# Transformer layer with self-attention, cross-attention and gated feed-forward: the heads of both batches as one stream, V projected four heads at a time, and the cross-attention of both batches in one pipeline ahead of both feed-forward parts

## The chip, the cores and the metric

The kernel runs on one core of one Trainium2 chip. The metric is device time in microseconds (us) from launch to end. TensorE is called PE in the profile, VectorE DVE, ScalarE ACT, GpSimd POOL, and SyncE, which issues most of the DMAs here, SP.

## What is computed

One layer on x of shape (2, 1024, 256), with 16 heads of 64 and a condition of (2, 64, 192):

```
h = layernorm(x, ln1); x = attention(h, h) + x            # self-attention, 1024 keys
h = layernorm(x, ln2); x = attention(h, cond_emb) + x     # cross-attention, 64 keys
h = layernorm(x, ln3); p = h @ ff_w1 + ff_b1              # (2, 1024, 2048)
a, gate = p[..., :1024], p[..., 1024:]
out = a * gelu(gate) @ ff_w2 + ff_b2 + x
```

Attention projects q, k and v to 1024 features, takes the softmax of q k^T / 8 for each head, multiplies by v, and projects back to 256 features. Everything is float32. Products that the kernel takes in fp32r split their operands into a high and a low part and add three terms (hi x hi, lo x hi, hi x lo), which `TERMS` lists.

## The kernel before, in words

Each engine has its own hand-written program, and semaphores tie the programs together. The order on every engine is fixed by these programs. Five tables of numbers place work inside the heads: `BURSTS`, `STEPS`, `TURNS`, `V_SLOT` and the function `proj_at`.

The whole program is a loop over the batch, `for b in range(B)`, on every engine. In each turn of it:

- **LayerNorm 1**: DVE takes statistics of x and centres it (L1000), PE turns the result (L522 `transpose_h`), ACT and DVE split it into hT_hi and hT_lo. While PE waits, it executes transposes without a use (L489 `keep_busy`).
- **First projections**: q and k of the first pair of heads (L534 `project`, six matmuls of 512 columns each), then V of all 16 heads in 16 items of six matmuls of 512 columns (L545 `project_v`). Six of them stand ahead of head 0 (`V_EARLY`), ten in its first five steps (`V_SLOT`). V goes to a scratch tensor in DRAM (SP L294) and comes back one head at a time (SP L239).
- **Heads**: a head is eight steps t, one for each tile of 128 keys. In a step PE makes the scores of 128 keys by 1024 queries (L561, 4 matmuls of 512 columns), DVE takes the row maximum (L1043), ACT the exponential (L840), DVE turns the tile in place (L1048). PE multiplies the tiles of the head before by V in two bursts, after the scores of t=2 and t=4 (L581 `attend`), 128 of its matmuls to a burst, ACT gathers the product (L848), PE projects it out in parts (L593) after t=5, 6, 7 and the next t=0, ACT scales it (L861), POOL adds it to X (L433). At t=7 and t=0 stand the projections of a later pair (L534), split by ACT (L811) and DVE (L1019). SP then moves the split q and k of a pair into the operands of its scores (L206, six transfers a head), in the order of its program: placing, V, weights and `wo` all go through this one queue.
- **After the heads**: PE combines the cross-attention's weights with the condition's keys and values (L614 `make_m`, L621 `make_vw`), LayerNorm 2 is done, then the cross-attention goes over eight tiles as a pipeline: scores of tile t (L722), DVE maximum, difference and sum (L1107 to L1121), POOL multiplies by the inverse sum (L471), PE turns tile t-2 (L732) and multiplies tile t-3 (L741).
- **Feed-forward**: in two halves of 512 tokens with 8 steps each: `SC<-hT` is the product with W1 (L770, 12 matmuls of 512 columns), ACT takes the gelu (L955), DVE multiplies (L1156) and splits (L1160), PE multiplies by W2 (L753, 12 matmuls of 256 columns) two steps later.

PSUM is divided in two score buffers `SC` of two banks each and `W` of four banks (TP[0], TP[1], PV, MISC), which all the rest shares.

## Time and profile before

| | |
|---|---|
| median of 3 runs | 1110.43 us (1109.74 to 1113.83) |
| profiled execution, its own time | 1112.73 us |
| its span (first to last instruction) | 1110.9 us |
| mean granted TensorE clock | 0.988 |
| instructions | 28351 |
| DMA moved | 124.52 MB, mean 112 GB/s |

The predictions of time are made against the profiled execution, whose own time is 1.83 us above its span. The page's line of busy times says how long each engine worked in the span. A window (a stretch from one time to another) gives the same for a part of it, and the timeline the single instructions, with what ended the idle time before them.

### The profile page before, as it was taken

The numbers are of one execution on the slowest core, as the hardware profiler recorded it, in microseconds if no ns is written. First come the engines' busy times: TensorE is split into PE (matmuls) and PEld (weight loads), VectorE is DVE, ScalarE is ACT, GpSimd is POOL, SyncE is SP. The second block draws the span as 40 slices with busy tenths as digits, with TensorE's granted clock in tenths as the row PEclk, the third lists the DMA queues.
The fourth block names the chain that finished last, engine by engine and source line by source line (L and its number), as shares of the span: only waits on it lengthen the run. The fifth ranks groups of instructions, "written<-read, shape, count | busy, mean of one in ns | idle before, by whom it ended". The sixth has DMA issues, their size and how long they took to land.

```text
span 1110.9 us, 28351 instructions
## 1 busy us (share of the span) xinstructions
PE 1051.9 (95%) x12178; PEld 846.3 (76%) x12178; DVE 860.5 (77%) x1024; ACT 600.9 (54%) x1082; POOL 333.0 (30%) x312
## 2 busy tenths in 40 slices
...
GB/s 179 295 227 149 146 116 122 144 118 160 102 157 184 99 47 31 39 67 1 19 53 247 202 117 149 116 133 166 108 130 147 144 130 120 21 19 38 1 20 19
DMA packets 178606, 124.52 MB, mean 112 GB/s; under 512 B 142768, under 2 KB 157616, under 8 KB 174128
## 3 DMA queue, kind: packets, MB, share of 16 engines
...
q14 instruction: 30, 0.25, 0.1%
...
## 4 chain that ended last, share of the span: by engine, by line
PE 67%; issue 15%; DVE 6%; POOL 5%; ACT 4%; SPq 2%; DMA 1%; POOLq 0%; DVEq 0%; ACTq 0%
PE W L581 15%; PE SC L561 13%; PE SC L770 8%; PE W L534 7%; PE W L593 7%; POOL X L433 4%; PE W L753 4%; PE W L741 3%; PE W L545 3%; PE SC L722 3%; ACT OTF L848 2%; SPq L206 2%; ACT PR L840 1%; PE W L732 1%; DVE PR L1000 1%
## 5 line engine op out<-in xcount | busy, mean ns | idle before, releaser
L840 ACT ACTIVATE PR<-SC,nmax 128x1024 f32<-128x1024 f32 x256 | 285.9, 1117 | 237.0 <-DVE nmax L1043 237.0
L1043 DVE TENSOR_REDUCE nmax<-SC 128x1 f32<-128x1024 f32 x256 | 307.6, 1201 | 84.3 <-PE SC L561 84.1
L1048 DVE STREAM_TRANSPOSE PR<-PR 128x1024 f32<-128x1024 f32 x256 | 314.9, 1230 | 0.2
L561 PE MATMUL SC<-QKS 128*128 128x512 f32 x1024 | 299.8, 419 | 11.3 <-ACT PR L840 9.0
L433 POOL TENSOR_TENSOR X<-f_raw,X 128x512 f32<-128x512 f32 x128 | 164.3, 1286 | 475.2 <-ACT f_raw L861 474.9
L561 PEld LDWEIGHTS SC<-QKS 128*128 128x128 f32 x1024 | 185.0, 188 | 80.9 <-ACT PR L840 24.6
L581 PE MATMUL W<-PR,V 32*64 32x256 f32 x8192 | 238.7, 377 | 0.5 <-issue 0.5
L581 PEld LDWEIGHTS W<-PR,V 32*64 32x64 f32 x8192 | 186.5, 131 | 46.5 <-issue 13.6
L593 PE MATMUL W<-wo,OTF 128*128 128x256 f32 x512 | 134.2, 385 | 7.8 <-ACT OTF L848 6.0
L593 PEld LDWEIGHTS W<-wo,OTF 128*128 128x128 f32 x512 | 93.6, 189 | 36.4 <-ACT OTF L848 20.0
L861 ACT ACTIVATE f_raw<-W,rden 128x256 f32<-128x256 f32 x256 | 106.7, 474 | 2.2 <-PE W L593 2.0
L1156 DVE SCALAR_TENSOR_TENSOR PR<-SC,b,PR 128x512 f32<-128x512 f32 x32 | 24.0, 750 | 69.2 <-ACT PR L955 69.2
L955 ACT ACTIVATE PR<-SC,b 128x512 f32<-128x512 f32 x32 | 22.1, 689 | 79.2 <-PE SC L770 79.1
L1019 DVE SCALAR_TENSOR_TENSOR QKT<-W,QKT 128x512 fp32r<-128x512 f32 x64 | 43.5, 685 | 13.2 <-ACT QKT L811 13.0
L931 ACT ACTIVATE PR<-PR 128x1024 f32<-128x1024 f32 x16 | 16.9, 1059 | 66.3 <-DVE PR L1111 66.3
L741 PE MATMUL W<-QKT,PT_hi 128*128 128x256 f32 x256 | 50.8, 299 | 0.0
L840 ACT ACTIVATION_READ_ACCUMULATOR PR<-SC,nmax 128x1 f32 x256 | 49.8, 195 | 0.0
L811 ACT ACTIVATE QKT<-W 128x512 fp32r<-128x512 f32 x64 | 38.2, 601 | 18.4 <-PE W L534 18.4
L534 PE MATMUL W<-hT_hi,w_hi 128*128 128x512 f32 x128 | 44.4, 428 | 0.8 <-DVE hT_lo L1011 0.8
L471 POOL TENSOR_TENSOR PR<-PR,crec 128x1024 f32<-128x1024 f32 x16 | 30.4, 1899 | 45.4 <-DVE crec L1121 45.4
L741 PEld LDWEIGHTS W<-QKT,PT_hi 128*128 128x128 f32 x256 | 42.3, 203 | 0.0
L848 ACT COPY OTF<-W 128x1024 f32<-128x1024 f32 x32 | 32.5, 1015 | 16.8 <-PE W L581 14.6
...
## 6 DMA issues: line engine op xcount, KB each, us to landing
...
V<-scratch_v SPq DMA_DIRECT2D x128, 256.0 KB, 4.8
QKS<-QKT SPq DMA_DIRECT2D x128, 128.0 KB, 4.7
...
```

Source lines behind the costliest of these rows:

```text
L433: nc.gpsimd.tensor_tensor(xs, f_raw[:, k % 2, :], xs, ALU.add).then_inc(p_x, 1)
L534: last = mm(bank, w_s[l][:, m, k, :], hT[r][:, k, half * BANK:(half + 1) * BANK], start=(c == 0 and k == 0), stop=(c == 2 and k == KD - 1))
L561: last = mm(SC[t % 2][:, cols], QKS[:, 3 * s, t * P:(t + 1) * P], QKS[:, 3 * s + 1 + l, cols], start=(l == 0), stop=(l == 1))
L581: last = mm(W[cols, a, 0:2 * P], V4[s][rows, blk, :], PR[rows, NT * s:NT * s + NT, Q * blk:Q * blk + Q], start=(blk < 2), stop=(blk >= NB ...
L593: last = mm(W[:, OUT_BANK[k], D * i:D * i + D], OTF[:, t * P:(t + 1) * P], wo2[h % 2][:, :], start=True, stop=True)
L741: last = mm((PV, MISC)[(t - 3) % 2][:, 0:D], PT[l][:, (2 * (t - 3) + n // 4) % NPT, (n % 4) * P:(n % 4 + 1) * P], VWx[r][:, n, :], start=( ...
L770: last = mm(SC[f % 2][:, part * BANK:(part + 1) * BANK], W1[l][:, k, col:col + P], hT[m][:, k, r * BANK:(r + 1) * BANK], start=(c == 0 and ...
L840: nc.scalar.activation(PR[:, NT * s + t, :], SC[t % 2][:, :], ACT.Exp, bias=nmax[:, t % 4:t % 4 + 1], accum_out=den[:, s, t:t + 1]).then_i ...
L848: nc.scalar.copy(OTF[:, :].rearrange("p (t a i) -> p a t i", a=4, i=Q), W[:, :, 0:2 * P].rearrange("p a (t i) -> p a t i", i=Q)).then_inc( ...
L861: done = nc.scalar.mul(f_raw[:, k % 2, D * i:D * i + D], W[:, OUT_BANK[k], D * i:D * i + D], rden[:, h % 2, 2 * k + i:2 * k + i + 1])
L1043: V.tensor_reduce(nmax[:, t % 4:t % 4 + 1], SC[t % 2][:, :], AX, ALU.max, negate=True).then_inc(d_max, 1)
L1048: V.transpose(tile, tile).then_inc(d_tr, 1)
```

## The change

The loop over the batch goes from every engine. In its place:

- The 32 heads of both batches (`HS`) are one stream. Pair g of 16 (`GS`) is projected from places given in `PROJ_AT`. Pairs 8 and 9, the first of batch 1, are projected in heads 13 to 16.
- V is projected in eight units of four heads (`US`). A unit has four items of 12 matmuls with 256 columns each. Unit 0 stands ahead of head 0, the others go one item to a head into the step after the scores of t=5 (`V_AT`); unit 4, the first of batch 1, has its four items in heads 14 and 15. SP stores an item (`store_v`), waits for the four of a unit (`stored`) and loads V for one head (`load_v`).
- LayerNorm 1 of batch 1 is spread over heads 10 to 14: statistics in head 10, aggregation in head 11, the square root on ACT at head 12, centring in head 12, turning and splitting in heads 13 and 14. Statistics of LayerNorm 2 of batch 0 are in heads 29 and 30.
- After the heads, `make_m` and `make_vw` are done for both batches. The cross-attention is one pipeline of 16 tiles. The feed-forward part follows as one loop of 32 steps, whose first two stand in the pipeline's last tiles. `LN_CA` and `LN_FF` place LayerNorm 2 and 3. `keep_busy` is left only at the start.
- W1 and W2 are loaded and split once, W_v comes in pieces of four heads. The gains of LayerNorm 2 and 3 are multiplied on ACT, not on DVE. x of batch 1 is loaded twice (1 MB each).

```diff
+NQ = 4
+def proj_of(g, n):
+    return ((("k", 0), ("q", 0), ("k", 1), ("q", 1)) if g % NP == 0 else
+            (("k", 0), ("k", 1), ("q", 0), ("q", 1)))[n]
+PROJ_AT = {(0, 5): [(1, 0, 3)], (0, 6): [(1, 1, 2)], (0, 7): [(1, 2, 1), (1, 3, 0)],
+           (13, 7): [(8, 0, 3)], (14, 0): [(8, 1, 2)], (14, 7): [(8, 2, 3), (8, 3, 2)],
+           (15, 6): [(9, 0, 2)], (15, 7): [(9, 1, 3)], (16, 0): [(9, 2, 2)], (16, 7): [(9, 3, 3)]}
+for g in range(2, GS):
+    if g not in (8, 9):
+        for n in range(NQ):
+            PROJ_AT[2 * (g - 2) + 1 + n // 2, 7 * (n % 2)] = [(g, n, 2 + n % 2)]
+V_AT = {(0, 4): (1, 0, 0), (14, 5): (4, 0, 3), (14, 6): (4, 1, 0), (15, 0): (4, 2, 0), (15, 5): (4, 3, 3)}
+for u in range(1, US):
+    if u != 4:
+        for i in range(4):
+            if u > 1 or i > 0:
+                V_AT[4 * (u - 1) + i, 5] = (u, i, 3)
+TURN_X = {(13, 0): [(0, 2), (1, 0)], (13, 5): [(2, 3)], (13, 6): [(3, 2)]}
+X_GAIN = {(13, 0): (0, 2), (13, 1): (1, 0), (13, 6): (2, 3), (13, 7): (3, 2)}
+X_HIGH = X_LOW = {(13, 1): 0, (13, 2): 1, (13, 7): 2, (14, 0): 3}
+TURN_W = {(HS - 3, 7): (0, 3), (HS - 2, 0): (1, 2), (HS - 2, 7): (2, 3), (HS - 1, 0): (3, 2)}
...
-V_EARLY = 6
-V_SLOT = {0: (6, 7), 1: (8, 9), 2: (10, 11), 3: (12, 13), 4: (14, 15)}
+LN_CA = {5: 2, 9: 3, 13: 4}
+LN_FF = {3: 5, 11: 6, 19: 7}
...
+def store_v(u, i):
+    sp.wait_ge(a_v, 4 * u + i + 1)
+    sp.dma_start(V_d[u % 2, :, 2 * i:2 * i + 2, :], VST[:, 2 * i:2 * i + 2, :]).then_inc(m_vst[i], 16)
+def stored(u):
+    for i in range(4):
+        sp.wait_ge(m_vst[i], 16 * (u + 1))
...
+for p in range(GS):
+    h = 2 * p
+    if p > 0:
+        for at in ((h - 1, 0), (h - 1, 5)):
+            if at in V_AT:
+                store_v(*V_AT[at][:2])
+        if p == NP - 1:
+            sp.wait_ge(s_tr, 8)
+            sp.dma_start(X[:, 1, :, :], by_row(x, 1)).then_inc(m_xb, 16)
+        sp.wait_ge(s_sc, NT * h)
+        place(p, 1)
+        if p + 2 < GS:
+            load_w(p + 2)
+        if p % 2 == 0:
+            stored(h // 4)
+            sp.wait_ge(s_pv, 8 * (h - 1))
+            load_v(h)
+        elif p // 2 + 2 < US:
+            load_wv(p // 2 + 2)
+        sp.wait_ge(s_op, 4 * (h - 1))
+        load_wo(h)
+        sp.wait_ge(s_pv, 8 * h)
+        load_v(h + 1)
+    if p == 1:
+        load_x(1)
+    for at in ((h, 4), (h, 5), (h, 6)):
+        if at in V_AT:
+            store_v(*V_AT[at][:2])
...
+    if p + 1 < GS:
+        sp.wait_ge(d_qkv, NQ * (p + 2))
+        sp.wait_ge(s_sc, NT * (h + 1))
+        place(p + 1, 0)
...
+    if (h + 2) % 4 and p + 1 < GS:
+        sp.wait_ge(s_pv, 8 * (h + 1))
+        load_v(h + 2)
...
+def project_v(u, i, bank):
+    if i == 0:
+        pe.wait_ge(p_wv, u + 1)
+    for j in range(2):
+        for c, (l, r) in enumerate(TERMS):
+            for k in range(KD):
+                last = mm(bank[:, 4 * DH * j:4 * DH * (j + 1)], hT[l][:, k, (2 * i + j) * P:(2 * i + j + 1) * P],
+                          wv_s[r][:, k, :], start=(c == 0 and k == 0), stop=(c == 2 and k == KD - 1))
+    last.then_inc(s_v, 1)
...
+for h in range(HS):
+    for t in range(NT):
+        scores(h, t)
+        if h > 0 and t in BURSTS:
+            attend(h - 1, BURSTS[t])
+        if h > 0 and t in STEPS:
+            if (h, t) == (NH - 2, 7):
+                pe.wait_ge(a_v, V_ISSUED[h] + 2)
+            project_out(h - 1, STEPS[t])
+        if (h, t) in V_AT:
+            u, i, bank = V_AT[h, t]
             if h == 0:
-                for i in V_SLOT.get(t, ()):
-                    project_v(i)
+                pe.wait_ge(a_v, 4)
+            elif t == 0:
+                pe.wait_ge(a_op, 4 * (h - 2) + 3)
+            project_v(u, i, W[:, bank, :])
...
-    pe.wait_ge(a_op, 4 * (H0 + NH))
-    keep_busy(MISC, 16)
-    pe.wait_ge(d_vw, 4 * b + 2)
-    transpose_h(L2, 0)
-    keep_busy(MISC, 8)
...
+make_m(0, 0, SCB[0])
+make_m(0, 1, SCB[1])
+attend(HS - 1, (0, NB))
+pe.wait_ge(a_exp, HS * NT)
+make_m(0, 2, SCB[2])
+make_m(0, 3, SCB[3])
+pe.wait_ge(d_m, 2)
+turn_z(0, SCB[0:2])
+for k in range(3):
+    project_out(HS - 1, k)
+pe.wait_ge(d_m, 4)
+turn_z(1, SCB[2:4])
+pe.wait_ge(a_op, 4 * (HS - 1) + 2)
+project_out(HS - 1, 3)
+for j in range(4):
+    if j > 0:
+        pe.wait_ge(a_op, 4 * (HS - 1) + (0, 1, 3, 4)[j])
+    make_m(1, j, MB[j])
+pe.wait_ge(a_ln, 2)
+ca_scores(0)
+pe.wait_ge(m_kvb[1], 16)
+pe.wait_ge(m_cao, 16)
+for j in range(4):
+    pe.wait_ge(d_m, 4 + j + 1)
+    make_vw(0, j, MB[j])
+pe.wait_ge(a_ln, 4)
+ca_scores(1)
+for j in range(4):
+    pe.wait_ge(d_vw, j + 1)
+    make_vw(1, j, MB[j])
...
+NC = B * NT
+for C in range(2, NC + 3):
+    if C < NC:
+        pe.wait_ge(d_cs, C - 1)
+        ca_scores(C)
+    elif C < NC + 2:
+        if C == NC:
+            pe.wait_ge(p_f, 8)
+        pe.wait_ge(d_cs, C - 1)
+        ff_up(C - NC)
...
+for F in range(2, B * 2 * NF + 2):
+    if F < B * 2 * NF:
+        pe.wait_ge(d_u, F - 1)
+        if F == 4:
+            pe.wait_ge(p_f, 12)
+        ff_up(F)
+    if F in LN_FF:
+        n = LN_FF[F]
+        if n == 5:
+            pe.wait_ge(d_cx, NC)
+        else:
+            pe.wait_ge(d_fx, 2 * (n - 5))
+        turn_z(n, TP if n == 6 else (PV, MISC))
+    if (F - 2) % NF == 0 and F > 2:
+        pe.wait_ge(a_ln, 2 * (4 + (F - 2) // NF) + 2)
+    ff_down(F - 2)
...
+        if h == NH - 6:
+            if t == 0:
+                for r in range(2):
+                    dve.wait_ge(m_x[r], 32)
+            stats(NT + t, X[:, 1, t, :], d_st)
+        if h == NH - 5:
+            if t == 0:
+                dve.wait_ge(d_st, 2 * NT)
+            aggr(NT + t, d_mv)
+        if (h, t) == (NH - 4, 1):
+            dve.wait_ge(a_sd, 3)
+            V.reciprocal(rs[:, NT:2 * NT], sd[:, NT:2 * NT]).then_inc(d_rs, 1)
+            dve.wait_ge(d_rs, 3)
+        if h == NH - 4 and 2 <= t < 6:
+            for i in (2 * t - 4, 2 * t - 3):
+                centre(X[:, 1, i, :], X[:, 1, i, :], NT + i, d_z)
```

The first place is the middle of a head on PE, after the second burst. Before, scores and output projections alternate (`L593` is the output projection, `L561` the scores, `L534` a projection of q or k):

```order
L581 MATMUL W<-PR,V_0 64x256 x64
L561 MATMUL SC<-QKS 128x512 x4
L593 MATMUL W<-wo_0,OTF 128x256 x2
L561 MATMUL SC<-QKS 128x512 x4
L593 MATMUL W<-wo_0,OTF 128x256 x2
L561 MATMUL SC<-QKS 128x512 x4
L593 MATMUL W<-wo_0,OTF 128x256 x2
```

After, the same place (`L613` is the burst, `L590` the scores, `L625` the output projection, `L575` V):

```order
L613 MATMUL W<-PR,V_1_63 64x256 x64
L590 MATMUL SC<-QKS 128x512 x4
L625 MATMUL W<-wo_1,OTF 128x256 x2
L575 MATMUL W<-wv_hi,hT_hi 128x256 x2
L575 MATMUL W<-wv_lo,hT_hi 128x256 x2
L575 MATMUL W<-wv_hi,hT_lo 128x256 x2
L575 MATMUL W<-wv_hi,hT_hi 128x256 x2
L575 MATMUL W<-wv_lo,hT_hi 128x256 x2
L575 MATMUL W<-wv_hi,hT_lo 128x256 x2
L590 MATMUL SC<-QKS 128x512 x4
L625 MATMUL W<-wo_1,OTF 128x256 x2
```

One item of V, 12 matmuls, has come between the output projection at t=5 and the scores of t=6; nothing else moved there.

The second place is PE after the last head. Before (`L614` is `make_m`, `L581` the whole of the last head's product, `L621` `make_vw`, `L489` `keep_busy`, `L522` the turning of LayerNorm 2, `L722` the first scores of the cross-attention):

```order
L614 MATMUL SC<-V_0,WQT 128x128 x8
L581 MATMUL W<-PR,V_1 64x256 x128
L614 MATMUL SC<-V_0,WQT 128x128 x4
L593 MATMUL W<-wo_1,OTF 128x256 x4
L614 MATMUL SC<-V_0,WQT 128x128 x4
L593 MATMUL W<-wo_1,OTF 128x256 x4
L621 MATMUL SC<-CAW,V_0 128x256 x8
L489 MATMUL W<-ident 128x128 x16
L522 MATMUL SC<-ident,PR 128x128 x8
L489 MATMUL W<-ident 128x128 x8
L722 MATMUL SC<-QKS,hT_hi 128x512 x4
```

After (`L642` is `make_m`, `L553` the turning, `L648` `make_vw`, `L666` the scores of the cross-attention):

```order
L642 MATMUL SC<-KV_0_64,WQT 128x128 x8
L613 MATMUL W<-PR,V_1_63 64x256 x128
L642 MATMUL SC<-KV_0_64,WQT 128x128 x8
L553 MATMUL SC<-ident,PR 128x128 x8
L625 MATMUL W<-wo_1,OTF 128x256 x6
L553 MATMUL SC<-ident,PR 128x128 x8
L625 MATMUL W<-wo_1,OTF 128x256 x2
L642 MATMUL W<-KV_0_64,WQT 128x128 x16
L666 MATMUL SC<-QKS,hT_hi 128x512 x4
L666 MATMUL SC<-QKS,hT_lo 128x512 x2
```

Both halves of LayerNorm 2 are turned between other work, the transposes without a use are gone, and `make_m` of batch 1 (x16) stands ahead of the first scores. `make_vw` of the two batches (x8 each) follows the scores of tile 0 and of tile 1.

The third place is ACT at the start of head 12, where the square root of batch 1's LayerNorm 1 is taken (`L909` is the exponential, `L928` the scaling, `L885` the high part of q or k, `L880` the square root):

```order
L909 ACTIVATE PR_49,den<-SC1,nmax 128x1024
L928 ACTIVATE f_raw<-W,rden 128x256 x2
L885 ACTIVATE QKT2_54<-W 128x512 x2
L880 ACT_TABLE_LOAD
L880 ACTIVATE sd<-mv 128x8
L909 ACT_TABLE_LOAD
L909 ACTIVATE PR_49,den<-SC0,nmax 128x1024
```

Two table loads and the root now stand inside the stream of exponentials; before, they stood between the batches.

## Rows read from the trace of the kernel before

**Rows 1.** The page: busy time, share of the span and instructions of each engine.

```profile
PE 1051.9 (95%) x12178; PEld 846.3 (76%) x12178; DVE 860.5 (77%) x1024; ACT 600.9 (54%) x1082; POOL 333.0 (30%) x312
```

**Rows 2.** Windows: one inner head, then the end of batch 0 to head 1.

```profile
core 0: us, PE busy (x) PEld busy (x) DVE busy (x) ACT busy (x) POOL busy (x), PEclk, DMA share, GB/s
94.61:116.74 22.13, 21.82 (x317) 16.70 (x316) 19.82 (x20) 14.57 (x27) 6.29 (x7) 1.00 0.46 94
...
381.25:407.58 26.33, 25.24 (x565) 20.80 (x564) 16.94 (x18) 12.78 (x25) 6.00 (x5) 1.00 0.25 77
407.58:423.15 15.57, 12.91 (x88) 11.40 (x81) 10.02 (x24) 10.30 (x19) 8.43 (x7) 1.00 0.17 52
423.15:448.47 25.32, 18.54 (x97) 15.51 (x97) 22.88 (x35) 8.88 (x12) 11.17 (x9) 0.93 0.07 21
448.47:474.36 25.89, 25.89 (x178) 23.71 (x176) 20.16 (x25) 6.98 (x10) 17.85 (x17) 1.00 0.11 35
...
490.13:559.84 69.71, 68.24 (x394) 60.01 (x393) 29.52 (x52) 23.27 (x37) 2.39 (x1) 1.00 0.02 8
559.84:588.80 28.96, 22.90 (x114) 19.60 (x113) 17.86 (x43) 8.34 (x14) 15.57 (x16) 0.88 0.35 87
588.80:620.63 31.83, 30.87 (x135) 24.97 (x135) 23.13 (x23) 18.12 (x33) 2.28 (x4) 1.00 1.06 265
...
1106.47:1110.90 4.43, 0.00 (x0) 0.00 (x0) 1.29 (x2) 0.00 (x0) 0.00 (x0) 0.71 0.29 118
```

**Rows 3.** Timeline of PE: start, duration; starts of head 0's and head 11's bursts.

```profile
72.55 3.71 PE L581 MATMUL W<-PR,V 32*64 32x256 f32 x128
...
316.31 3.71 PE L581 MATMUL W<-PR,V 32*64 32x256 f32 x128
```

**Rows 4.** Timeline of PE: one feed-forward step, two products with W1.

```profile
499.24 0.28 PE L753 MATMUL W<-W_hi,PT_hi 128*128 128x256 f32 x1
...
500.68 0.63 PE L770 MATMUL SC<-hT_hi,W_hi 128*128 128x512 f32 x2
...
504.86 0.63 PE L770 MATMUL SC<-hT_hi,W_hi 128*128 128x512 f32 x2
```

**Rows 5.** Timeline of DVE: row maxima of tiles 0 and 8, and two in head 7.

```profile
41.95 1.23 DVE L1043 TENSOR_REDUCE nmax<-SC 128x1 f32<-128x1024 f32 x1 [0.21 <-PE SC L561]
...
68.24 1.22 DVE L1043 TENSOR_REDUCE nmax<-SC 128x1 f32<-128x1024 f32 x1
...
218.66 1.19 DVE L1043 TENSOR_REDUCE nmax<-SC 128x1 f32<-128x1024 f32 x1
...
220.91 1.19 DVE L1043 TENSOR_REDUCE nmax<-SC 128x1 f32<-128x1024 f32 x1
```

**Rows 6.** Timeline of PE: half of `make_m`, `make_vw`, half of a `transpose_h`.

```profile
410.80 1.05 PE L614 MATMUL SC<-V,WQT 128*128 128x128 f32 x8
...
413.42 3.62 PE L621 MATMUL SC<-CAW,V 128*128 128x256 f32 x16
...
495.63 1.04 PE L522 MATMUL W<-ident,PR 128*128 128x128 f32 x8
```

**Rows 7.** Timeline of ACT: a table load and the activation after it.

```profile
493.15 1.28 ACT L955 ACT_TABLE_LOAD   x1 [0.30 <-PE SC L770]
494.45 0.69 ACT L955 ACTIVATE PR<-SC,b 128x512 f32<-128x512 f32 x1
```

**Rows 8.** Timeline of DVE: cross-attention's steady tile, and statistics of four tiles.

```profile
457.93 1.23 DVE L1107 TENSOR_REDUCE cmax<-SC 128x16 f32<-128x1024 f32 x1 [0.80 <-PE SC L722]
...
480.10 1.40 DVE L989 BATCH_NORM_STATS2 st<-X 128x6 f32<-128x256 f32 x4
```

**Rows 9.** Groups by line: weight loads of one operand pair of W2.

```profile
L753 PEld LDWEIGHTS W<-W_lo,PT_hi 128*128 128x128 f32 x128 | 24.5, 191 | 0.9
```

**Rows 10.** Timeline of SP's queue and PE: placing for batch 1's first scores.

```profile
580.54 7.13 SPq L206 DMA_DIRECT2D QKS<-QKT  x6
...
588.80 1.17 PE L561 MATMUL SC<-QKS 128*128 128x512 f32 x4 [1.48 <-DMA QKS<-QKT]
```

More of the change, by code:

```diff
@@ L59, in build_block @@
+        fence = sb("fence", [P, 36 * S])
+        X = sb("X", [P, B, NT, D])
         hT = [sb("hT_hi", [P, KD, S], F32R), sb("hT_lo", [P, KD, S], F32R)]
-        QKS = sb("QKS", [P, 6, S], F32R)
-        V4 = [sb(f"V4_{h}", [P, NB, DH]) for h in range(2)]
         OTF = sb("OTF", [P, S])
@@ new lines, in ff_up @@
+            def ff_up(F):
+                q, f = divmod(F, NF)
+                if f == 0:
+                    pe.wait_ge(d_ll, 2 * (4 + q) + 2)
+                for part, col in enumerate((FF + f * P, f * P)):
+                    for c, (l, m) in enumerate(TERMS):
+                        for k in range(KD):
+                            last = mm(SC[F % 2][:, part * BANK:(part + 1) * BANK], W1[l][:, k, col:col + P],
+                                      hT[m][:, k, by_col(q)], start=(c == 0 and k == 0), stop=(c == 2 and k == KD - 1))
+                last.then_inc(s_ff, 1)
@@ new lines, in ff_down @@
+            def ff_down(F):
+                q, f = divmod(F, NF)
+                pe.wait_ge(d_ul, F + 1)
+                for i in range(4):
+                    bank = ((TP[0], TP[1]), (PV, MISC))[q % 2][i // 2]
+                    for c, (l, m) in enumerate(TERMS):
+                        last = mm(bank[:, D * (i % 2):D * (i % 2) + D], PT[l][:, F % NPT, i * P:(i + 1) * P],
+                                  W2[m][:, f, :], start=(f == 0 and c == 0 and i % 2 == 0),
+                                  stop=(f == NF - 1 and c == 2), skip_group_check=True)
+                last.then_inc(s_w2, 1)
@@ new lines, in ca_exp @@
+            def ca_exp(C):
+                act.wait_ge(d_cs, C + 1)
+                nc.scalar.activation(E[C % 4], E[C % 4], ACT.Exp).then_inc(a_ce, 1)
+            for r in range(2):
+                act.wait_ge(d_mv, 4 * r + 4)
+                root(by_tile(r), a_sd)
+            for r in range(2):
+                for k in range(2):
+                    act.wait_ge(d_h, 2 * r + k + 1)
+                    nc.scalar.copy(hT[0][:, k, by_col(r)], h32[:, k, by_col(r)]).then_inc(a_hh, 1)
+            raw_kv(0)
```

1561 lines of the change are left out of this document (765 added, 796 removed).

## The prediction

> **What bounds the kernel now.** I read the busy times first [rows 1]: PE works 95% of the span, DVE 77%. Of 1110.9 us PE is idle for 59.0, so whatever is to be won beyond that must come from work that is dropped. The windows then say where the idle time is [rows 2]. An inner head lasts 22.13 us, PE busy for 21.82 of it and DVE for 19.82: in the heads PE is the bound, and DVE is close behind. The idle time is elsewhere. From the end of the last head's bursts to the steady cross-attention PE idles 15.57 - 12.91 = 2.66 and 25.32 - 18.54 = 6.78 us, and between the end of batch 0 and its successor's first scores 28.96 - 22.90 = 6.06 us. The reader should also see what that busy time holds: in these stretches PE executes transposes without a use, and its first projections and six V items, while no exponential runs. Head 0 with ten V items takes 31.83 us to the next burst [rows 2], nearly all PE time. The gain of the change is the second start, 28.96 + 31.83 = 60.8 us, and the second entry into the cross-attention, less what is put into the heads.
>
> **The heads.** From the burst of head 0 to that of head 11 are 11 heads in 316.31 - 72.55 us, 22.16 each [rows 3]. The stream has 30 such intervals between the bursts of head 0 and head 30: 30 x 22.16 = 664.8. All but two hold the same two projections as before or the turning of the cross-attention's weights, so I leave them at that.
>
> V is added. In the feed-forward part 12 matmuls of 256 columns, also with loaded weights of 128x128 and three terms, take from 499.24 to 500.68, 1.44 us; the step of 4.18 us less 1.44 leaves 2.74 for 12 of 512 columns, so an item of before costs 1.37 and one of after 1.44 [rows 4]. After unit 0 and the item in head 0, 27 items stand in the stream. Since PE is the bound there, each costs its whole time less the little that it already idles (0.31 us a head [rows 2]): I take 1.43, near the upper bound of 1.44, because the waits in a head are at other places than the V item; the lower bound is 1.44 - 0.31 - the 0.6 or so by which a longer head lets waits on ACT and DVE vanish, about 0.6. The sum is 27 x 1.43 = 38.6. DVE gets nothing of it (V is copied by ACT), and at 23.6 us a head DVE has 3.8 us left.
>
> LayerNorm 1 of batch 1 has four turnings of four transposes in head 13, and the row of two such has 1.04 us with the drain of its last, so some 0.45 each and 1.8 for four [rows 6]. With a wait of 0.4 at each I take 3.4 for all, bounds 1.6 and 6. Its DVE work, eight statistics at 1.40/4 = 0.35 [rows 8] and some 20 more small operations over five heads, lies in DVE's free time. The root at head 12 brings two table loads of 1.28 us, and the activation behind one starts 1.30 us after it [rows 7]. They delay one exponential by about 2.8 us; PE is two tiles ahead of it, with a row maximum every 2.25 us [rows 5], and most of that wait is filled by the projection and output at t=0. I take 0.8, bounds 0 and 2.8. The Trainium skill ("ScalarE: Activation LUTs", section "What ACT_TABLE_LOAD costs") has a switch cost 2.66 us, a load of 1283 ns and a drain of 1380 ns. The row shows the 1.28 and no drain behind it; by the page the sum would be 2.7 us longer, some 1080 instead of 1077. The stream so takes 664.8 + 38.6 + 3.4 + 0.8 = 707.6 us.
>
> **The start.** Before, 72.55 us pass to the first burst [rows 3]. Ahead of head 0 stand four items instead of six, 2 x 1.37 less; its first row maximum is at 41.95 [rows 5] and would come at 39.6 (I give the four items of new form 0.4 more). From tile 0 to tile 8 before are 68.24 - 41.95 = 26.29 us, because two V items stand in each early step; without them DVE sets the pace, with 8 x 2.25 and splits of 0.7 behind two tiles, 19.5. The first burst follows 72.55 - 68.24 = 4.3 us later, as before. Together 39.6 + 19.5 + 4.3 = 63.4; bounds 60 (nothing of the early DMA is late) and 67 (the second placing is late, where the DMA engines now work at a share of 1.06 [rows 2]).
>
> **After the heads.** From head 30's burst to the end of head 31's: 26.33 before [rows 2], 26.3 after. Then to the fifth tile's scores before 15.57 + 25.32 = 40.9 us, of which PE idles 9.4 and has 24 transposes without a use, 0.1 each going by an x8 row less its drain, 2.4. The change adds M and V·W of batch 1: two rows of 1.05, less a drain 0.9 each, and 3.62, less its drain 3.5, 5.3 together [rows 6]. They fit the idle time and the dropped 2.4, but the chain that made PE wait (statistics, root, centring, turning, splitting on DVE) is still there, only earlier: half of its LayerNorm 2 statistics is done in heads 29 and 30. I take 41; bounds 34 (all idle time used) and 46 (nothing hidden). Twelve more tiles at 25.89/4 = 6.5 us [rows 2] are 78.0; three turnings of LayerNorm 2 and 3 at 0.9 [rows 6] are 2.7. DVE idles 0.80 us in a tile [rows 8], and nine extra pieces of DVE work of about 1.4 us each (four centrings of a half, three splits, two statistics of 1.40) are put into the twelve tiles: 12.6 against 9.6 free, so 3.0 of stalls, bounds 0 and 9 x (1.4 - 0.8) = 5.4, up to 10 if a delay also reaches POOL's multiplication. The tail of the pipeline has two turnings at 0.8 and three products of 24 matmuls at 1.44/12 = 0.12 [rows 4], 10.2. The joined feed-forward part is twice 69.71 [rows 2] and 1.8 for two more turnings, 141.2. The end stays 4.4 [rows 2].
>
> Sum: 63.4 + 707.6 + 26.3 + 41.0 + 78.0 + 2.7 + 3.0 + 10.2 + 141.2 + 4.4 = 1077.8, against a span of 1110.9. With the 1.8 us outside the span 1079.6 against the execution's own 1112.7; the median of the runs is 2.3 less, so 1077 us.
>
> What costs nothing: W1 and W2 split once instead of twice spares POOL alone, which is busy for 30% [rows 1]; storing V in 32 pieces, and reading x again, are transfers beside the heads, where the DMA engines have a share of 0.46 [rows 2]. If that cover is gone, the price is rival D's.
>
> **The rivals.**
>
> A. V is paced by its weight loads. One takes 191 ns [rows 9], and an item has 12 now instead of six. If loads of full height didn't overlap more than one deep here, an item would take 12 x 0.191 = 2.29 us, 0.85 more: 32 x 0.83 = 27 us, and 1104. Against it stands the pitch of 0.12 us at which the feed-forward part runs with the same loads [rows 4, 9]. The Trainium skill speaks for it: "TensorE: Matmul & The Clock Gate", section "The mechanism", says that a weight load overlaps running matmuls only where the row group differs, and these all fill the rows. By that rule the stride of 0.12 couldn't be, so the trace disagrees. Chance 0.05.
>
> B. The heads absorb V. If a longer head lets PE's waits on ACT and the weight loads' gaps vanish, an item costs 0.9 to 1.0 instead of 1.43: 27 x 0.48 = 13 less, 1064. For it: the 22.13 us of a head hold only 16.70 of weight loads [rows 2], so the busy PE is not PE at its peak. Against it: it is busy for 21.82 of 22.13. Chance 0.12.
>
> C. The seams cost more: the start at its upper bound (+4), LayerNorm in head 13 and the tables (+4), the entry into the cross-attention (+5), the stalls (+5). Any two or three of them give 1087 to 1095. Chance 0.10, more likely through the cross-attention, where DVE is nearly full.
>
> D. Slower: SP's queue. It places q and k for a head when the head before it has left its slot, issues them for 7.13 us, and the one place where PE was seen to wait for them cost 1.48 us [rows 10]. The queue now has `store_v` ahead of the placing and `stored` ahead of V's loads, and each wait holds all behind it. If placing came late in every head, it costs per head what it is late: at 1.1 us a head the gain of 33 is gone, at 1.3 the kernel is slower by over 0.5%; at 1.48 in 30 heads it is +44, 1121. Against it: the item in step 5 of a head is copied by ACT within two steps, and the placing waits for step 8 anyway; the issue takes 7.13 us of the 23.6 that a slot has, and a landing behind it of as much again still leaves 9. Chance 0.04.
>
> **How the numbers follow.** The forecast has 0.69, so 1077 us. A measurement of this kernel can tell about 0.5%, that is 1105 to 1116 for no change. A, which ends just at that border, gives most of "same" and the upper half of D "slower"; B and C are faster. So faster 0.92, same 0.04, slower 0.04. The range leaves out A and D and the far ends of B and C: below, 1077 less 13 for V and 2 for the start, 1062; above, 1077 and the unknown costs of C together, 20, 1097.
>
> **What would show it.** Right: the interval between bursts in heads 1 to 10 is 23.5 to 23.7 us, V's 12 matmuls take 1.4 to 1.5 from first to next instruction, head 12 is less than 3 us longer, the first burst is at 60 to 67, the pipeline's tiles come every 6.5 to 7 us, the feed-forward step every 4.18. Wrong: the interval at 24.4 or more with weight loads as cause (A); at 23.1 or less (B); DVE as releaser of PE in the cross-attention with tiles of 7 and more (C); the scores waiting for QKS at t=0 or t=4 of many heads (D). A granted clock below the 1.00 of the heads in the stream would also break the sum.

## The result: 3.6% slower, and the profile after

The changed kernel took 1150.92 us (median of 4 runs, 1147.97 to 1156.53) against 1111.97 us (1109.74 to 1113.83) of the kernel before: a ratio of 1.0357, 95% interval 1.0305 to 1.0409. The forecast was 1077 us with a range of 1062 to 1097, and a chance of 0.04 for slower. The forecast missed by 74 us, and the sign with it. The profiled span is 1146.5 us, to be held against the forecast sum of 1077.8.

The page of the changed kernel, busy times:

```profile
PE 1055.1 (92%) x12270; PEld 841.2 (73%) x12270; DVE 859.3 (75%) x997; ACT 605.5 (53%) x1094; POOL 308.4 (27%) x280
```

PE has about the work that it had [rows 1], 1055.1 us against 1051.9. It now idles 91 us instead of 59 (span less busy time). PE's busy time hardly grew, and part of the growth is work at a lowered clock (below); what is new is that PE waits. For what, the view of the waits of PE tells (engine and line that wait, the instruction waited for, us in total, times, longest):

```profile
PE W L565 <- ACT VST L892: 25.5, 24, 1.1
PE W L826 <- POOL PR L498: 14.7, 7, 3.5
PE SC L590 <- ACT PR L909: 11.3, 8, 2.9
PE W L553 <- DVE PT_lo L1296: 7.3, 3, 3.3
PE W L625 <- ACT OTF L917: 6.7, 27, 0.7
PE W L648 <- DVE M_lo L1115: 3.9, 1, 3.9
PE W L613 <- DVE hc L1106: 3.6, 1, 3.6
```

The first row is new in kind and the largest: 24 times 1.1 us, the projection of q or k (L565) waits for ACT's copy of V (L892). The second row is not new: in the kernel before it is `PE W L732 <- POOL PR L471: 15.3, 6, 3.5`. The windows of one inner head, of the interval between bursts that holds the two table loads, of the head with LayerNorm 1 of batch 1, of the entry into the cross-attention, of its tiles 4 to 15, and of the rest:

```profile
core 0: us, PE busy (x) PEld busy (x) DVE busy (x) ACT busy (x) POOL busy (x), PEclk, DMA share, GB/s
...
236.96:261.86 24.90, 23.50 (x330) 18.05 (x329) 19.90 (x20) 14.93 (x28) 8.11 (x9) 1.00 0.72 144
312.07:339.91 27.84, 23.58 (x330) 18.06 (x329) 22.28 (x28) 18.32 (x32) 6.22 (x7) 1.00 0.56 124
365.99:394.12 28.13, 26.11 (x324) 18.95 (x324) 20.94 (x22) 14.90 (x28) 4.22 (x4) 0.90 0.67 150
838.66:884.96 46.30, 36.85 (x200) 31.50 (x201) 34.99 (x51) 23.64 (x41) 15.51 (x11) 0.93 0.11 34
884.96:988.11 103.15, 88.02 (x555) 78.68 (x553) 85.23 (x118) 32.63 (x49) 50.32 (x38) 0.93 0.06 19
988.11:1146.50 158.39, 148.04 (x880) 130.82 (x880) 70.08 (x122) 53.79 (x87) 20.22 (x16) 1.00 0.05 19
```

The inner head [rows 2, 22.13 us] now takes 24.90, where 23.6 was forecast. Of its 24.90 us PE is busy for 23.50: the head has become longer by 2.77 us, of which 1.68 is busy time of PE and 1.09 waiting. The stretches add up like this (us):

| stretch | forecast | changed kernel | difference | best version, below |
|---|---|---|---|---|
| start to first burst | 63.4 | 62.7 | -0.7 | 63.7 |
| 30 heads, burst to burst | 707.6 | 749.6 | +42.0 | 714.5 |
| last head | 26.3 | 26.4 | +0.1 | 26.4 |
| entry, to scores of tile 4 | 41.0 | 46.3 | +5.3 | 39.7 |
| tiles 4 to 15 | 83.7 | 103.2 | +19.5 | 91.3 |
| feed-forward and end | 155.8 | 158.4 | +2.6 | 157.1 |
| span | 1077.8 | 1146.5 | +68.7 | 1092.7 |

Three rows hold nearly the whole miss, 66.8 of 68.7 us: heads, entry, tiles.

### The profile page after: what moved, and what is told of

Its sections match the earlier page's. It is cut to its first block, busy times and chain, and to the rows that moved or that the text cites. A ratio compares the mean times of both kernels' runs of the same rounds, so it can differ in the third digit from the quotient of the medians.

```text
span 1146.5 us, 28589 instructions
## 1 busy us (share of the span) xinstructions
PE 1055.1 (92%) x12270; PEld 841.2 (73%) x12270; DVE 859.3 (75%) x997; ACT 605.5 (53%) x1094; POOL 308.4 (27%) x280
## 4 chain that ended last, share of the span: by engine, by line
PE 57%; issue 16%; DVE 12%; ACT 8%; POOL 4%; SPq 2%; DMA 1%; ACTq 0%; DVEq 0%; POOLq 0%
PE W L613 15%; PE SC L590 11%; PE SC L678 7%; PE W L565 7%; PE W L688 4%; DVE nmax L1128 4%; PE W L575 4%; PE W L625 3%; POOL X L447 3%; ACT OTF L917 2%; ACT PR L909 2%; ACT f_raw L928 2%; PE W L835 2%; SPq L230 1%; DVE PR L1133 1%
## 5 line engine op out<-in xcount | busy, mean ns | idle before, releaser
L909 ACT ACTIVATE PR<-SC,nmax 128x1024 f32<-128x1024 f32 x256 | 286.2, 1118 | 260.7 <-DVE nmax L1128 260.6
L590 PE MATMUL SC<-QKS 128*128 128x512 f32 x1024 | 295.6, 415 | 12.3 <-ACT PR L909 11.3
L613 PE MATMUL W<-PR,V 32*64 32x256 f32 x8192 | 241.6, 381 | 3.8 <-DVE hc L1106 3.6
L590 PEld LDWEIGHTS SC<-QKS 128*128 128x128 f32 x1024 | 182.7, 188 | 82.7 <-ACT PR L909 29.1
L613 PEld LDWEIGHTS W<-PR,V 32*64 32x64 f32 x8192 | 186.7, 132 | 52.5 <-issue 17.9
L625 PE MATMUL W<-wo,OTF 128*128 128x256 f32 x512 | 134.6, 385 | 10.1 <-ACT OTF L917 6.7
L625 PEld LDWEIGHTS W<-wo,OTF 128*128 128x128 f32 x512 | 93.6, 189 | 39.0 <-ACT OTF L917 20.6
L928 ACT ACTIVATE f_raw<-W,rden 128x256 f32<-128x256 f32 x256 | 107.0, 478 | 1.9 <-PE W L625 1.2
L1328 DVE SCALAR_TENSOR_TENSOR GU<-SC,b,GU 128x512 f32<-128x512 f32 x32 | 23.9, 750 | 70.5 <-ACT GU L1053 70.5
L565 PE MATMUL W<-hT_hi,w_hi 128*128 128x512 f32 x128 | 43.8, 424 | 27.1 <-ACT VST L892 25.5
L1053 ACT ACTIVATE GU<-SC,b 128x512 f32<-128x512 f32 x32 | 21.9, 687 | 82.3 <-PE SC L678 82.3
L885 ACT ACTIVATE QKT<-W 128x512 fp32r<-128x512 f32 x64 | 38.2, 598 | 48.0 <-PE W L565 48.0
L565 PEld LDWEIGHTS W<-hT_hi,w_hi 128*128 128x128 f32 x128 | 21.9, 188 | 41.5 <-ACT VST L892 35.2
L909 ACT ACTIVATION_READ_ACCUMULATOR PR<-SC,nmax 128x1 f32 x256 | 50.2, 196 | 0.0
L678 PE MATMUL SC<-hT_hi,W_hi 128*128 128x512 f32 x128 | 40.1, 395 | 2.1 <-DVE GU L1328 1.2
L435 POOL TENSOR_TENSOR X<-X,bias_row 128x1024 f32<-128x1024 f32 x12 | 29.9, 2502 | 37.5 <-DVE PR L1090 37.5
```

The source lines that it names most:

```text
L565: last = mm(bank, w_s[l][:, m, k, :], hT[r][:, k, half * BANK:(half + 1) * BANK], start=(c == 0 and k == 0), stop=(c == 2 and k == KD - 1))
L590: last = mm(SC[t % 2][:, cols], QKS[:, 3 * s, t * P:(t + 1) * P], QKS[:, 3 * s + 1 + l, cols], start=(l == 0), stop=(l == 1))
L613: last = mm(W[cols, a, 0:2 * P], V4[s][rows, blk, :], PR[rows, NT * s:NT * s + NT, Q * blk:Q * blk + Q], start=(blk < 2), stop=(blk >= NB ...
L625: last = mm(W[:, OUT_BANK[k], D * i:D * i + D], OTF[:, t * P:(t + 1) * P], wo2[h % 2][:, :], start=True, stop=True)
L678: last = mm(SC[F % 2][:, part * BANK:(part + 1) * BANK], W1[l][:, k, col:col + P], hT[m][:, k, by_col(q)], start=(c == 0 and k == 0), stop ...
L909: nc.scalar.activation(PR[:, NT * s + t, :], SC[t % 2][:, :], ACT.Exp, bias=nmax[:, t % 4:t % 4 + 1], accum_out=den[:, s, t:t + 1]).then_i ...
```

## Experiments

Ten kernels were run, each timed beside the kernel before on the same chip. Those with a ratio compute the whole layer and have four to six executions. The other three (the second, the fourth and the ninth) leave something out and were executed once; from them only stretches of their one profile are read. Spans and stretches are those of single profiled executions, which differ by a few us from one execution of a kernel to the next. The first four edits are to the changed kernel; the later runs build on the first and the third, as each says.

### Where V is copied

ACT's program empties the PSUM bank of a V item of step 5 ahead of the exponential of tile 7. The timeline of ACT in the changed kernel, behind the exponential of tile 6 of a head:

```profile
252.49 1.11 ACT L909 ACTIVATE PR<-SC,nmax 128x1024 f32<-128x1024 f32 x1 [1.79 <-DVE nmax L1128]
...
253.59 0.83 ACT L928 ACTIVATE f_raw<-W,rden 128x256 f32<-128x256 f32 x2
254.30 0.59 ACT L892 COPY VST<-W 128x512 f32<-128x512 f32 x1
```

and of PE in the same head:

```profile
249.86 0.40 PE L575 MATMUL W<-wv_hi,hT_lo 128*128 128x256 f32 x2
250.10 1.09 PE L590 MATMUL SC<-QKS 128*128 128x512 f32 x4
...
252.82 1.03 PE L625 MATMUL W<-wo,OTF 128*128 128x256 f32 x4
254.95 0.73 PE L565 MATMUL W<-hT_hi,w_hi 128*128 128x512 f32 x2 [1.10 <-ACT VST L892]
```

V is done at 250.10, ACT idles 1.79 us up to 252.49, and copies it only at 254.30, because its program has the exponential first, which waits for a maximum of scores that PE made after V. The projection at t=7 (L565) goes into the same bank. The edit puts the copy ahead of the exponential of tile 6 (`v_before` names, for a tile, the items that ACT copies ahead of its exponential):

```diff
-    at = {0: [(h, 0)], 6: [(h, 4)], 7: [(h, 5), (h, 6)]}.get(t, [])
+    at = {0: [(h, 0)], 6: [(h, 4), (h, 5)], 7: [(h, 6)]}.get(t, [])
```

> The changed kernel, with one thing moved: ACT copies the V item of step 5 of a head ahead of the exponential of tile 6 and not ahead of that of tile 7. Nothing is left out. Theory 1 (the V item's bank is the cause: the projection at t=7 goes to the same PSUM bank, and PE waits 1.10 us in each of 24 heads for ACT's copy, which stands behind the exponential of tile 6): the waits PE L565 <- ACT VST vanish, the interval between bursts falls from 24.9 to 23.8 us, the span from 1146.5 to about 1121. Theory 2 (PE is held by its work and by the chain of maximum and exponential, and the wait is only where that slack shows): the same idle time comes back at the scores or at the output projection, interval 24.6 or more, span 1140 or more.

Measured: 1118.99 us, ratio 1.0039 (1.0020 to 1.0059); span 1117.0, 29.5 less. The waits for VST are gone from the view, and the window of an inner head, from burst to burst, reads

```profile
228.01:251.57 23.56, 23.26 (x330) 18.15 (x329) 19.91 (x20) 15.02 (x28) 8.06 (x9) 1.00 0.69 143
```

Intervals of 23.45 and 23.56 us alternate; from the burst of head 1 to that of head 9 the mean is 23.50 ((275.02 - 87.00) / 8), 1.34 over the 22.16 of before [rows 3]. The forecast's 1.43 for an item was nearly right, on the condition that the bank is emptied in time. Theory 1 holds; the gain is 1.4 us a head, the wait and 0.3 more. Over the 30 intervals it is 32.8 us (780.23 - 63.51 = 716.7 against 749.6); start and end of this execution were 3.3 us longer than in the other, which is about what single executions differ by. With this one move the kernel is still 0.4% slower than the one before, clear of noise: the wait for V is the largest cause, and not the only one.

The second run turns the question round: nearly all of V's matmuls go, the copy stays where it was.

```diff
-    for c, (l, r) in enumerate(TERMS):
-        for k in range(KD):
-            last = mm(bank[:, 4 * DH * j:4 * DH * (j + 1)], hT[l][:, k, (2 * i + j) * P:(2 * i + j + 1) * P],
-                      wv_s[r][:, k, :], start=(c == 0 and k == 0), stop=(c == 2 and k == KD - 1))
+    last = mm(bank[:, 4 * DH * j:4 * DH * (j + 1)], hT[0][:, 0, (2 * i + j) * P:(2 * i + j + 1) * P],
+              wv_s[0][:, 0, :], start=True, stop=True)
```

> The changed kernel with 10 of the 12 matmuls of every V item left out (V is not computed; ACT's copy, the stores and loads stay). Takes 1.2 us of PE work from each item. Theory 1 (the copy's place sets the end): everything behind the item moves up by 1.2 us, the wait for the copy stays at about 1.1, interval 23.7 us, span 1146.5 - 32 x 1.2 = 1108. Theory 2 (V's PE work costs more than its own time, by its weight loads or by slack lost): interval 22.3, span about 1070.

Measured: span 1125.9 (one execution), 20.6 less, not the 38 of the first theory's span; but the interval of a head is 23.63 to 23.73 us, as it says, 1.2 less, and the wait is all there:

```profile
PE W L565 <- ACT VST L890: 25.5, 23, 1.2
```

From the burst of head 0 to that of head 27 it is 22.2 us less (721.86 - 60.51 against 746.24 - 62.69), where 24 heads with an item at 1.2 would be 29. Of the rest, 4.4 us are three idle times of PE in the first heads for which the profile names no releaser (1.83 before scores at 66.05, 1.23 and 1.36 before bursts at 72.89 and 116.44; why they are there stays open), and a wait for a copy of V at 403.25 is 2.23 us where the changed kernel has 1.0. Ten of 12 matmuls left out gain less than one copy moved. The wait depends on the chain of scores, maximum and exponential, not on V's work: theory 2 falls.

### POOL and DVE

DVE's timeline at the entry into the cross-attention, changed kernel, and POOL's of the same stretch:

```profile
845.12 1.29 DVE L1160 TENSOR_TENSOR hT_lo<-PR,hT_hi 128x512 fp32r<-128x512 f32 x2 [3.14 <-ACT hT_hi L955]
850.50 6.45 DVE L1160 TENSOR_TENSOR hT_lo<-PR,hT_hi 128x512 fp32r<-128x512 f32 x2 [4.08 <-ACT hT_hi L955]
856.88 2.47 DVE L1115 TENSOR_TENSOR M_lo<-W,M_hi 128x512 fp32r<-128x512 f32 x4
```

```profile
850.10 1.58 POOL L404 DMA_DIRECT2D f_raw<-in_L_xattn_ff_w_dram  x2
851.70 4.69 POOL L435 TENSOR_TENSOR X<-X,bias_row 128x1024 f32<-128x1024 f32 x2
```

The same pair of splits takes 1.29 us once and 6.45 the next time, and ends at 856.95, where POOL's addition ends at 856.39. PE waits 3.85 us for what stands behind it on DVE. That the addition on POOL holds DVE up is so far only a coincidence in time. The test moves POOL's additions:

```diff
-add_bias_ln(0)
-add_bias_ln(1)
 for C in range(B * NT):
...
-    if C in (5, 9, 13, 15):
-        add_bias_ln({5: 2, 9: 3, 13: 4, 15: 5}[C])
+    if C in (0, 1, 4, 8, 12, 15):
+        add_bias_ln({0: 0, 1: 1, 4: 2, 8: 3, 12: 4, 15: 5}[C])
```

> The changed kernel with POOL's additions of the bias (L435, 2.3 to 2.8 us each) moved: behind the multiplications of tiles 0, 1, 4, 8, 12 and 15 instead of ahead of tile 0 (two) and behind 5, 9, 13, 15. Nothing is left out. Theory 1 (DVE's subtraction of two SBUF operands, L1160, can't run while POOL's addition runs: 6.45 us for two at 850.5 and 3.93 at 909 and 945, against 1.29): the splits take 1.3 each, PE's wait of 3.85 us for M_lo falls under 1, the stall of tile 8 to 9, 13 to 14 (2.6 and 4.2 us) shrinks; span 6 to 12 us less. Theory 2 (the stalls come from the turning's wait for the TP banks and from DVE being full): the splits may shorten, the span falls by less than 3.

Measured: 1138.27 us, ratio 1.0226 (1.0207 to 1.0246); span 1133.6, 12.9 less. The split and the entry as a window:

```profile
851.79 1.29 DVE L1158 TENSOR_TENSOR hT_lo<-PR,hT_hi 128x512 fp32r<-128x512 f32 x2 [4.08 <-ACT hT_hi L953]
```

```profile
839.94:879.67 39.73, 35.35 (x200) 30.74 (x201) 29.63 (x51) 23.75 (x41) 15.46 (x11) 0.96 0.13 40
```

The entry takes 39.7 us instead of 46.3, where 41 was forecast. The tiles 4 to 15 fall from 103.2 to 95.2. Both sides of theory 1 came out, the operation and the wait; the 12.9 lie just above its 6 to 12. The Trainium skill ("VectorE: DVE Perf Modes", section "Two Vector instructions with no wait between them") has an instruction with two SBUF tensor inputs read the second through an interface that it shares with GpSimd. The trace agrees as far as it goes: L1160, both inputs in SBUF, ends 0.56 us after POOL's addition of 4.69 us, while in the changed kernel L1296, one input in PSUM, takes its 1.29 us for two beside a multiplication on POOL:

```profile
908.02 1.29 DVE L1296 TENSOR_TENSOR PT_lo<-W,PT_hi 128x512 fp32r<-128x512 f32 x2 [0.18 <-ACT PT_hi L1043]
```

```profile
907.91 1.91 POOL L498 TENSOR_TENSOR PR<-PR,crec 128x1024 f32<-128x1024 f32 x1 [7.42 <-DVE crec L1188]
```

### The root at head 12

```diff
 def root(cols, signal):
+    if cols.start == NT and signal is a_sd:
+        nc.scalar.activation(sd[:, cols], mv[:, cols, 1], ACT.Exp, bias=EPS).then_inc(signal, 1)
+        return
```

> The changed kernel with the square root of batch 1's LayerNorm 1 replaced by an exponential, which needs no table load (the deviation of batch 1 is not computed). The interval of head 11 is 27.84 us in the changed kernel, 2.9 over its neighbours of 24.9. Theory 1 (the two table loads and the root delay one exponential by 2.8 us and nothing covers it): the interval falls to 25.0 to 25.3, span 2.5 to 2.9 less. Theory 2 (the cover holds, and the 2.9 are the centring and statistics on DVE): under 1 us less.

Measured: the interval falls from 27.84 to 24.96 us, by 2.88, as theory 1 says of it. The span does not follow: this one execution has 1148.5, 2.0 more than the changed kernel and not 2.5 to 2.9 less. Its first burst is 1.6 us later, the interval of head 0 is 0.7 longer, and over all 30 intervals it is only 1.0 us shorter (812.87 - 64.32 = 748.55 against 749.56). So what the loads cost at their place is shown, their share of the whole time is not. ACT in the changed kernel shows why the cover failed:

```profile
334.08 0.60 ACT L885 ACTIVATE QKT<-W 128x512 fp32r<-128x512 f32 x1 [1.70 <-PE W L565]
334.70 1.28 ACT L880 ACT_TABLE_LOAD   x1
335.99 0.21 ACT L880 ACTIVATE sd<-mv 128x8 f32<-128x8 f32 x1
336.22 1.28 ACT L909 ACT_TABLE_LOAD   x1
337.51 1.11 ACT L909 ACTIVATE PR<-SC,nmax 128x1024 f32<-128x1024 f32 x1
```

Two loads and the root are 2.8 us in a row, and the next scores wait 2.9 for the exponential (longest in the row `PE SC L590 <- ACT PR L909` above). No idle time stands between a load and what follows, so the drain that the Trainium skill adds ("ScalarE: Activation LUTs", "What ACT_TABLE_LOAD costs") is not seen; the loads' own time isn't covered either.

### Both moves together

> The changed kernel with the two moves of the first runs together: V's copy ahead of the exponential of tile 6, POOL's bias additions at other tiles. Nothing is left out. Theory 1 (two separate causes): the gains add up, 29.5 + 12.9, span about 1104, some 0.6% faster than the kernel before. Theory 2 (they share slack): 1110 or more.

Measured: 1104.11 us, ratio 0.992 (0.9893 to 0.9947), span 1101.6. The two gains, 29.5 and 12.9, add up to 42.4 and the two together gave 44.9. The causes are separate, and the kernel is now 0.8% faster than the one before.

### One buffer, and a wait that costs twice

In head 13 PE waits for DVE to empty a PSUM bank with turned x of batch 1, since DVE's buffer `hc` is still in use. Timeline and window of the burst behind it in the changed kernel:

```profile
365.99 6.56 PE L613 MATMUL W<-PR,V 32*64 32x256 f32 x128 [3.57 <-DVE hc L1106]
```

```profile
365.99:372.41 6.42, 6.42 (x128) 4.48 (x128) 2.71 (x3) 1.71 (x3) 0.00 (x0) 0.54 0.51 114
```

The granted clock of these 6.42 us is 0.54, near the lower of the two levels (1.2 GHz of 2.4), after 3.57 us of idle. In other heads a burst takes 3.71 [rows 3].

```diff
-hc = sb("hc", [P, BANK])
+hc = sb("hc", [P, 2, BANK])
...
-X_GAIN = {(13, 0): (0, 2), (13, 1): (1, 0), (13, 6): (2, 3), (13, 7): (3, 2)}
+X_GAIN = {(13, 0): [(0, 2), (1, 0)], (13, 6): [(2, 3)], (13, 7): [(3, 2)]}
```

> The run before this one, and a second buffer hc for the turned x of batch 1, so that DVE empties both PSUM banks at t=0 of head 13 and the burst needn't wait for the second (3.57 us in the changed kernel with V's copy moved, and the burst behind it took 6.42 us instead of 3.71). Nothing is left out. Theory 1 (the wait costs itself and, through a lowered clock, 2.7 us of the burst): the burst takes 3.71 again, span 5 to 6.5 less than with one buffer. Theory 2 (the long burst is DVE's or the operand's doing, and only the wait goes): 2.5 to 3.6 less.

Measured: 1101.69 us, ratio 0.9903 (0.9868 to 0.9938), span 1098.1, 3.5 less. The place itself does what theory 1 says:

```profile
348.92 3.71 PE L611 MATMUL W<-PR,V 32*64 32x256 f32 x128 [0.44 <-DVE hc L1104]
```

From the burst of head 10 to that of head 13 it is 6.05 us less than with one buffer (374.63 - 299.55 = 75.08 against 381.12 - 299.99 = 81.13). 2.4 us came back between the bursts of heads 28 and 30 (46.42 against 44.02): the windows show a granted clock of 0.97 and 0.96 there, against 1.00, with 1.93 us at 0.55 behind a wait of 1.60. Whether that belongs to the edit is open: two later runs that hold it too have 46.49 us and 44.81 in this stretch, the run with V's copy moved alone 44.28. The cause at the place is shown, the total is not settled between the theories.

### The turnings in the pipeline

LayerNorm 2 and 3 are turned on PE inside the tiles. In the run with both moves PE waits there for the two banks that the turning of the exponential also uses (8.0 us in three places). The next edit, on the run with both moves, uses the output bank that is idle:

```diff
-if C in LN_CA:
-    pe.wait_ge(d_cl, 2 * (C - 2) + 2)
-    turn_z(LN_CA[C], TP)
+for k in range(2):
+    if C - k in LN_CA:
+        n = LN_CA[C - k]
+        pe.wait_ge(d_lz, 4 * n + 4)
+        pe.wait_ge(d_cx, C - 3)
+        turn_rows((PV, MISC)[(C - 2) % 2], z, n % 2, k).then_inc(s_ln, 1)
```

The gain (ACT) and the split (DVE) of a half follow it, one half to a tile.

> The run with both moves, and the three turnings of LayerNorm inside the cross-attention's pipeline put into the output bank that is idle (one half in each of two tiles) instead of the two banks of the exponential's turning, for which PE waited 7.3 to 8.0 us in three places. Nothing is left out. Theory 1 (the shared banks make PE wait, and the three tiles last 9.4 to 12.3 us instead of 6.5): the waits PE L553 <- DVE PT_lo vanish, span 7 to 12 less than with both moves alone. Theory 2 (DVE is full, and the extra work of it sets the pace wherever PE waits): the waits appear at other places, under 3 less.

Measured: 1103.09 us, ratio 0.9911 (0.9877 to 0.9944), span 1103.0: no gain over 1101.6, as theory 2 has it. The waits for the banks are gone, and others stand there:

```profile
PE SC L676 <- DVE hT_lo L1314: 5.7, 1, 5.7
...
PE SC L664 <- DVE hT_lo L1314: 2.9, 1, 2.9
PE SC L664 <- issue: 2.8, 1, 2.8
```

From the end of the last product to the first feed-forward step it is even longer, 137.6 us against 134.9.

All four together:

> All four moves in one kernel: V's copy, POOL's bias additions, two buffers for x of batch 1, turning in idle banks. Nothing is left out. If each cause is its own: span about 1090, 2% faster than the kernel before. If the later ones share their slack: 1098 to 1104.

Measured: 1099.58 us, ratio 0.9887 (0.9861 to 0.9913), span 1100.8, the second of the two cases. Two runs then asked whether DVE's load or the order of the chain sets these tiles. They start from different kernels. The first cuts DVE's work and leaves its place (on the run with both moves):

```diff
+w = 32 if 2 <= n < 6 else D
...
-    centre(z[:, t, :], X[:, b, t, :], NT * b + t, d_lz)
+    centre(z[:, t, 0:w], X[:, b, t, 0:w], NT * b + t, d_lz)
```

> The run with both moves (span 1101.6; 134.9 us from the end of the last head's product to the first feed-forward step, of which 16 tiles at 6.5 would be 104), with DVE's LayerNorm work inside the pipeline cut to an eighth: centring of four halves, three splits, the statistics of LayerNorm 3 of batch 0 on 32 columns (their values are not those of the layer). All waits, PE's turnings and ACT's gains stay. Theory 1 (DVE is full and its extra 13 us of work against 0.8 us free a tile set the pace): the stretch falls by 8 to 10, to 125 to 127. Theory 2 (the chain of the turning, PE waiting for the last split, then ACT's gain ahead of the next turning, sets it, whatever DVE's load): 131 or more.

Measured: from the end of the last product (808.89) to the first feed-forward step (942.12) 133.2 us, against 134.9 with the full work: 1.7 less, where theory 1 had 8 to 10 and theory 2 "131 or more". But the edit cut the columns to an eighth or less, and not the time. In the groups of DVE from 845 to 944 us, the centring takes 588 ns a piece on 32 columns where it took 700 on 256:

```profile
L1088 DVE TENSOR_SCALAR PR<-X,mv,rs 128x256 f32<-128x256 f32 x16 | 10.2, 700 | 0.1
```

```profile
L1088 DVE TENSOR_SCALAR PR<-X,mv,rs 128x32 f32<-128x32 f32 x16 | 8.4, 588 | 0.1
```

With splits and statistics DVE's work of LayerNorm there fell from 18.6 to 12.0 us, by 6.6 and not by 11. And PE was busy for 2.1 us more in this stretch, at a granted clock of 0.95 against 0.97. So 6.6 us less work on DVE gave 1.7 us, up to 3.8 if the clock had been equal (an estimate, 1.7 + 2.1). Theory 1 is not borne out in its size, but the run doesn't clear DVE's load.

The second is the run with all four moves, with two turnings placed a tile earlier:

```diff
-LN_CA = {5: 2, 9: 3, 13: 4}
+LN_CA = {4: 2, 8: 3, 13: 4}
```

> The run with all four moves, with the first two turnings a tile earlier (after tiles 4 and 8, not 5 and 9). Nothing is left out. Turning in idle banks took away the 8 us of waits for the banks and gave 8.7 us of waits for the split of the second half (PE L664 and L676 <- DVE hT_lo) in their place. Theory 1 (the second half came a tile too late): the waits at tiles 8 and 12 vanish, span 3 to 6 us under 1100.8, 1095 to 1098. Theory 2 (DVE's load sets it): within 2 us of 1100.8.

Measured: 1094.62 us, ratio 0.9823 (0.9801 to 0.9845), span 1092.7, 8.1 less than the same kernel with the turnings a tile later; by the medians it is 5.0, and the two ratios (0.9823 and 0.9887) stand clear of each other. The stretch to the feed-forward part is 131.0 us, against 137.8 with all four moves and 134.9 with the first two: of the 6.8 us gained here, the turning in idle banks had lost 2.9 before. The waits at tiles 8 and 12 are gone, that of 5.7 at the first feed-forward step stays, since its turning wasn't moved:

```profile
935.63 1.19 PE L676 MATMUL SC<-hT_hi,W_hi 128*128 128x512 f32 x2 [5.69 <-DVE hT_lo L1314]
```

It is of the kind of V's copy. ACT has the high part of the second half done at 924.76, but DVE's program has the next tile's centring, maximum and sum ahead of the split:

```profile
923.84 2.67 DVE L1314 TENSOR_TENSOR hT_lo<-PR,hT_hi 128x512 fp32r<-128x512 f32 x1
...
926.77 2.37 DVE L1103 TENSOR_SCALAR PR<-X,mv,rs 128x256 f32<-128x256 f32 x4
...
934.34 1.15 DVE L1314 TENSOR_TENSOR hT_lo<-PR,hT_hi 128x512 fp32r<-128x512 f32 x1
```

No run moved this split. The six splits also take longer in these kernels, 1.40 us each against 0.98 in the run with both moves: L1314 has two SBUF inputs, and the first one above runs beside POOL's multiplication at 924.01. How much of the 131.0 us that costs was not tried.

This is the best version: 1.8% faster than the kernel before, and by the two medians 4.9% faster than the changed one (1094.62 / 1150.92 = 0.951).

## Why the prediction was wrong

**"PE is the bound there, each costs its whole time" (V in the heads, 27 x 1.43 = 38.6).** This step failed first of all. The item's price was nearly right (1.34 measured once the copy is in time); what was left out is the wait that the item brings. I took "V is copied by ACT" to mean only that DVE is spared, and did not ask what is queued ahead of the copy on ACT and what waits for the bank behind it. The two rows of the code that decide were both in view: the item writes bank 3 at t=5, the projection of t=7 writes bank 3. Rival D even says that the item "is copied by ACT within two steps"; two steps are all the time that the bank has. It cost 32.8 us in the heads, 29.5 in the span, which is nearly the 33 us of the forecast gain. By itself it would have made the forecast "same"; that the kernel came out slower took the other misses too, and the run with this one cause mended is still 0.4% slower than the kernel before. This was none of my rivals. Rival D was the wait in the wrong queue, SP's placing: the view of the waits of PE has none for a transfer.

**Table loads, "I take 0.8, bounds 0 and 2.8".** Mis-sized: 2.88. Two tiles of lead don't cover it, since PE may write the next scores only when the exponential two tiles back is done: it waits 2.93 us for that at 338.77.

**LayerNorm 1 of batch 1, "I take 3.4, bounds 1.6 and 6".** Mis-sized by about 9. In the run with V's copy moved, head 10's burst to head 16's took 155.97 us (299.02 to 454.99). Six intervals at 22.16, six items at 1.34 and 2.9 for the tables are 143.9, so some 12 us are left for this term (an estimate from these numbers). The wait in head 13 and the lowered clock behind it are 6.05 of them; which waits make up the rest was not tested. Even the best version has 6.9 us more than forecast in the 30 heads.

**"I take 41" for the entry.** Right without the contention (39.7), wrong with it (46.3). Rows of the kernel before had the sign of it, and I didn't look. There the second pair of splits, beside POOL's multiplication from 434.08 to 435.98, took 2.23 us, and the first 1.41:

```profile
421.68 1.41 DVE L1011 TENSOR_TENSOR hT_lo<-PR,hT_hi 128x512 fp32r<-128x512 f32 x2
...
435.32 2.23 DVE L1011 TENSOR_TENSOR hT_lo<-PR,hT_hi 128x512 fp32r<-128x512 f32 x2
```

**"3.0 of stalls, bounds 0 and 5.4, up to 10" in the tiles.** It was 22.5. The working counted DVE's extra work against its free time and took each piece at its length without POOL. 8.0 of the 22.5 was contention with POOL, 3.9 the bank and the tile of the turnings (95.2 against 91.3). The other 10.6 stand in the best version still; 5.7 of them are its last wait for a split, and how the rest divides between DVE's load and the order of its program is open. Rival C named the right place ("more likely through the cross-attention"), at less than half the size (5 for the entry and 5 for the stalls, against 24.8) and for DVE's fullness. Its sum is off as well: its terms are 4, 4, 5 and 5, so two or three of them give 1085 to 1091 and not 1087 to 1095, and all four 1095.

**What held.** The start (62.7 against 63.4), the last head (26.4 against 26.3), the feed-forward part (158.4 against 155.8, its step 4.18 as before), and rival A's rejection: V's 12 matmuls go from 248.48 to the next scores at 250.10 in 1.62 us, the first pair 0.42 and the others 0.24 each. That is a little over the 1.4 to 1.5 that I gave as the sign, and far from the 2.29 of rival A. Rival B does not hold either: an item costs 1.34, not 0.9 to 1.0.

Was the idea behind the change worth anything? With its waits mended the same order of work gives 0.9823: of the 33 us forecast, 18 are there (1110.9 to 1092.7 in span).
